# The last two of seven output groups of a graph attention layer computed on Pool instead of VectorE

## The chip, the cores and the metric

One core of a Trainium2 chip runs the whole program. The metric is the device time of one execution in microseconds. Durations inside an execution come from one profiled run, whose span goes from its first to its last instruction.

## The reference

One pre-normalised graph attention layer over 12500 nodes of 128 features and 200000 edges, with 4 heads of 32 features:

```python
h = jnp.maximum(_layernorm(x, axis=-1), 0.0)
h = (h @ W_node.T).reshape(num_nodes, H, HD)
e = (edge_features @ W_edge.T).reshape(num_edges, H, HD)
att = leaky_relu(sum(concat(h[src], h[tgt], e) * a))
m = jnp.maximum(segment_max(att, tgt), 0.0)
ex = jnp.exp(att - m[tgt])
denom = segment_sum(ex, tgt) + (num_edges - deg)[:, None] * jnp.exp(-m)
h_prime = segment_sum((ex / denom[tgt])[:, :, None] * h[src], tgt)
return x + h_prime.reshape(num_nodes, H * HD)
```

## The kernel before

The nodes are padded to 98 blocks of 128 (`N_BLOCKS`), one node per partition in each block. The program has three stages, each an `nc.Block()` in which every engine has a list of instructions written out by hand, ordered between engines by semaphores alone.

- **Stage 1** (lines 130 to 593) normalises and projects the nodes, writes a table of node rows to HBM, and lays the edges out in 1664 slots. Pool clears buffers here: some small `memset` calls and one of `vals` at the start (lines 234 to 242), one of 2375 words a partition (L248) and one of 11188 (L253). VectorE makes the statistics (`BN_STATS`, L275 and others), copies projected rows out of PSUM (L292) and computes what the slots need.
- **Stage 2** (lines 612 to 1125) goes through 52 groups of 32 slots. Pool issues an indirect DMA per slot that gathers source rows (L722), VectorE makes the scores, running maxima and weighted rows, TensorE sums them by node (L802), and VectorE adds each sum to `acc` (L1092). `acc` holds for each block a row of 137 words: per head 32 weighted sums, the sum of weights and the weight of the zero score, and after the four heads the node's degree.
- **Stage 3** (lines 1128 to 1175) is where the change lies. VectorE makes the denominators from `acc` (L1159 to L1165) and their reciprocals (L1167) in `den`, a part of `vals`. Then it goes through `N_OUT` = 7 groups of 14 blocks: it multiplies the group's sums in `acc` by the reciprocals, broadcast over the 32 features of a head, into `y`, a part of `onehot_b` (L1170), and adds `y` to that group's piece of `x`, in place (L1174). Each piece is 128 partitions by 1792 words, 896 KB.

The pieces of x lie in `x_again[g]`, buffers of stage 2 that are free by then: groups 0 and 1 in `eattr`, 2, 3, 5 and 6 in `gath`, 4 in `onehot_b`. Groups 0 to 4 are loaded from SyncE's queue (SP) before stage 2 ends, groups 5 and 6 at the start of stage 3 (L1145). ScalarE's queue (ACT) stores each group after its addition (L1151) and waits at the end for all seven stores. Pool has no instruction in stage 3. A semaphore wait stands between each two of VectorE's instructions here (`s_m`, `s_y`), since each reads what the one ahead wrote.

Of the kernel before, what the change touches and what calls it, by code (L numbers as in the profile page):

```python
# [13 lines left out]
HEADS, HD = 4, 32  # L14
P = 128
# [14 lines left out]
HC = HD + 2  # L30
# [13 lines left out]
def gat_kernel(nc, x, tiles, tile_ends, ea, w_node, w_edge, a, out):  # L44
    f32, bf16, i32 = mybir.dt.float32, mybir.dt.bfloat16, mybir.dt.int32
    ALU = mybir.AluOpType
# [10 lines left out]
    with ctx:  # L57
# [6 lines left out]
        def sem(name):  # L64
            return ctx.enter_context(nc.semaphore(name))
# [3 lines left out]
        acc_b = acc[:, :].rearrange("p (b c) -> p b c", c=ACC)  # L69
# [60 lines left out]
        with ExitStack() as stage:  # L130
            def ssem(name):
                return stage.enter_context(nc.semaphore(name))

            def ssb(name, shape, dt):
                return stage.enter_context(nc.sbuf_tensor(name, shape, dt))
# [38 lines left out]
            span, real, cnt, tot, before, end, slot_block, block, block128, same_block, unit, carry_in = (t13[:, i, :] for i in range(12))  # L174
# [19 lines left out]
            with nc.Block() as block_:  # L194
                @block_.sync
                def _(sp):
                    def load(g):
                        if g >= XBUF:
                            sp.wait_ge(n_["hn"], g - XBUF + 1)
                        sp.dma_start(xg[g % XBUF], x_g[g, :, :, :]).then_inc(s_x[g % XBUF], 16)  # L200

                    def store(g):
                        sp.wait_ge(n_["rows_act"], g + 1)
                        sp.wait_ge(n_["rows_dve"], g + 1)
                        sp.dma_start(tab_g[g, :, :, :], rows[:, g % 2, :, 0:ROW]).then_inc(s_rows[g % 2], 16)

                    sp.dma_start(ends_i[:, :, :], tile_ends).then_inc(s_ends, 16)
                    for g in range(XBUF):
                        load(g)
                    for g in range(N_NODE_GROUPS):  # L210
                        if g + XBUF < N_NODE_GROUPS:
                            load(g + XBUF)
                        if g == 2:
                            sp.wait_ge(s_block, 1)
                            sp.dma_start(slot_blocks.rearrange("(c p) -> p c", p=P), block_i[:, :], allow_slow_non_contiguous=True).then_inc(s_bstored, 16)
                        if g == 4:
                            sp.wait_ge(s_bstored, 16)
                            sp.dma_start(block_row[:, :], slot_blocks.rearrange("(o n) -> o n", o=1)).then_inc(s_brow, 16)
                        if g == FLAGS_AT:
                            sp.wait_ge(s_flags, 1)  # L220
                            sp.dma_start(flags.rearrange("e (c q) (s x) -> (q s) (e c) x", q=CG, x=4),
                                         chunk_flags[:, :, :, :].rearrange("p e c x -> p (e c) x")).then_inc(s_flags_out, 16)
                        store(g)
                    for q in range(2):
                        sp.wait_ge(s_rows[q], 16 * (N_NODE_GROUPS // 2))
                    sp.wait_ge(s_flags_out, 16)
                    sp.wait_ge(s_brow, 16)
# [270 lines left out]
                def _(pe):  # L498
# [96 lines left out]
        OW = 2 * NODE_GROUP  # L595
        N_OUT = N_BLOCKS // OW
        EARLY = 5
        FLAT = OW * NODE_DIM
        row_half = G * ROW
        x_again = [ea_flat[:, 0:FLAT], ea_flat[:, FLAT:2 * FLAT], gath_flat[:, 0:FLAT], gath_flat[:, FLAT:2 * FLAT],  # L600
                   oh_flat[:, 0:FLAT], gath_flat[:, row_half:row_half + FLAT], gath_flat[:, row_half + FLAT:row_half + 2 * FLAT]]
        x_again = [t.rearrange("p (w d) -> p w d", w=OW) for t in x_again]
        x_out = x.rearrange("(g i p) d -> g p i d", i=OW, p=P)
        s_again = [sem(f"x_again{g}") for g in range(N_OUT)]
# [9 lines left out]
        with ExitStack() as stage:  # L614
# [38 lines left out]
            with nc.Block() as block:  # L653
                @block.sync
                def _(sp):
# [35 lines left out]
                    def finish(g):  # L691
                        sp.wait_ge(s["vals"], 2 * g.n)
                        for n in range(2, EARLY - 1):
                            sp.dma_start(x_again[n], x_out[n, :, :, :]).then_inc(s_again[n], 16)
                        sp.wait_ge(s["cast"], 2 * NB * g.n)
                        sp.dma_start(x_again[EARLY - 1], x_out[EARLY - 1, :, :, :]).then_inc(s_again[EARLY - 1], 16)

# [234 lines left out]
                def _(dve):  # L932
# [128 lines left out]
                    def load_blocks(g, a):  # L1061
                        blocks = []
                        for part in range(GS // 8):
                            _, b = nc.values_load_multi_w_load_instructions(
                                block_row[:, ds(g.n * G + a * GS + 8 * part, 8)], engines=[mybir.EngineType.DVE], min_val=0,
                                max_val=N_BLOCKS, skip_runtime_bounds_check_because="clamped to N_BLOCKS in stage 1")
                            blocks += b
                        return blocks
# [59 lines left out]
        with ExitStack() as stage:  # L1128
            def ssem(name):
                return stage.enter_context(nc.semaphore(name))  # L1130

            def ssb(name, shape, dt):
                return stage.enter_context(nc.sbuf_tensor(name, shape, dt))

            y = oh_flat[:, G * P // 2:G * P // 2 + FLAT].rearrange("p (w d) -> p w d", w=OW)
            y_flat = oh_flat[:, G * P // 2:G * P // 2 + FLAT]
            den, inv = (vals_flat[:, n * 512:n * 512 + N_BLOCKS * HEADS] for n in range(2))
            den3, inv3 = (t.rearrange("p (b h) -> p b h", h=HEADS) for t in (den, inv))
            s_e, s_d, s_r, s_m, s_y, s_out = (ssem(n) for n in ("empty_nodes", "denominators", "reciprocals", "normalised", "results", "stored"))
            out_g = out.rearrange("(g i p) d -> g p i d", i=OW, p=P)  # L1140
            with nc.Block() as block:
                @block.sync
                def _(sp):
                    for g in range(EARLY, N_OUT):
                        sp.dma_start(x_again[g], x_out[g, :, :, :]).then_inc(s_again[g], 16)  # L1145

                @block.scalar
                def _(act):
                    for g in range(N_OUT):
                        act.wait_ge(s_y, g + 1)  # L1150
                        act.dma_start(out_g[g, :, :, :], x_again[g]).then_inc(s_out, 16)  # L1151
                    act.wait_ge(s_out, 16 * N_OUT)

                @block.vector
                def _(dve):
                    V = nc.vector
                    a_all = acc_b[:, 0:N_BLOCKS, 0:HEADS * HC].rearrange("p b (h c) -> p b h c", h=HEADS)
                    others = y_flat[:, 0:N_BLOCKS]
                    V.tensor_scalar(others, acc_b[:, 0:N_BLOCKS, HEADS * HC], -1.0, float(N_EDGES), ALU.mult, ALU.add).then_inc(s_e, 1)  # L1159
                    dve.wait_ge(s_e, 1)  # L1160
                    V.tensor_tensor(inv3, a_all[:, :, :, HD + 1], others.unsqueeze(2).broadcast_to((P, N_BLOCKS, HEADS)), ALU.mult).then_inc(s_e, 1)  # L1161
                    dve.wait_ge(s_e, 2)
                    V.tensor_tensor(den3, a_all[:, :, :, HD], inv3, ALU.add).then_inc(s_d, 1)  # L1163
                    dve.wait_ge(s_d, 1)
                    V.scalar_tensor_tensor(out=inv, in0=den, scalar=0.0, in1=den, op0=ALU.is_equal, op1=ALU.add).then_inc(s_d, 1)  # L1165
                    dve.wait_ge(s_d, 2)
                    V.reciprocal(den, inv).then_inc(s_r, 1)  # L1167
                    dve.wait_ge(s_r, 1)
                    for g in range(N_OUT):
                        V.tensor_tensor(y.rearrange("p b (h c) -> p b h c", h=HEADS), a_all[:, g * OW:(g + 1) * OW, :, 0:HD],  # L1170
                                        den3[:, g * OW:(g + 1) * OW, :].unsqueeze(3).broadcast_to((P, OW, HEADS, HD)), ALU.mult).then_inc(s_m, 1)
                        dve.wait_ge(s_m, g + 1)
                        dve.wait_ge(s_again[g], 16)
                        V.tensor_tensor(x_again[g], y, x_again[g], ALU.add).then_inc(s_y, 1)  # L1174
                        dve.wait_ge(s_y, g + 1)
# [34 lines left out]
```

## Time and profile before

| | us |
|---|---|
| median of 3 runs (2319.57 to 2323.26) | 2321.58 |
| the profiled execution | 2322.31 |
| its span, first to last instruction | 2320.5 |
| outside its span | 1.81 |
| stage 3 from its first instruction at 2281.4 to the span's end | 39.1 |

The engines are VectorE (DVE in the rows), ScalarE (ACT), GpSimd (POOL), SyncE (SP) and TensorE (PE, with its weight loads as PEld). A name with q behind it is an engine's queue, where DMAs are issued: the time of such a row is that of issuing, not of the transfer. A group of instructions is named by its line, its engine, its operation, what it writes and what it reads, by the program's buffer names: `onehot_b<-acc,vals` on L1170 is the product `y`, and `gath<-onehot_b,gath` on L1174 the sum with a piece of x.

### The profile page before, as it was taken

The numbers are of one execution on the slowest core, as the hardware profiler recorded it, in microseconds if no ns is written. First come the engines' busy times: TensorE is split into PE (matmuls) and PEld (weight loads), VectorE is DVE, ScalarE is ACT, GpSimd is POOL, SyncE is SP. The second block draws the span as 40 slices with busy tenths as digits, with TensorE's granted clock in tenths as the row PEclk, the third lists the DMA queues.
The fourth block names the chain that finished last, engine by engine and source line by source line (L and its number), as shares of the span: only waits on it lengthen the run. The fifth ranks groups of instructions, "written<-read, shape, count | busy, mean of one in ns | idle before, by whom it ended". The sixth has DMA issues, their size and how long they took to land. (4 is left out here: it accounts for less than half of the span.)

```text
span 2320.5 us, 28553 instructions
## 1 busy us (share of the span) xinstructions
PE 1202.7 (52%) x8210; PEld 996.3 (43%) x8210; DVE 1610.4 (69%) x4470; ACT 620.6 (27%) x1185; POOL 1623.3 (70%) x1711
## 2 busy tenths in 40 slices
PE   4465535555545546455455556555455554454441
PEld 4433434444444434444444344444344444443441
DVE  7426757767767767677677677677676776776777
ACT  5613212222222222222122222222222221222220
POOL 3077777777777777777777777777777777777730
PEclk9777677677767767767677777677677776666665
DMA  6554233233333333323233323323333222223235
GB/s 118 117 188 125 73 77 93 75 84 87 82 89 74 93 78 93 77 73 94 77 93 74 96 74 93 78 74 93 77 93 77 76 56 57 55 55 89 55 77 143
DMA packets 126702, 200.45 MB, mean 86 GB/s; under 512 B 35409, under 2 KB 92401, under 8 KB 120274
## 3 DMA queue, kind: packets, MB, share of 16 engines
q0 software_dynamic: 54912, 117.69, 22.0%
q1 hardware_dynamic: 58098, 74.36, 10.7%
q10 hardware_dynamic: 13536, 6.56, 1.0%
q8 instruction: 68, 1.11, 0.2%
q14 instruction: 88, 0.72, 0.1%
HBM read 182.18 MB, written 16.32 MB: 86 GB/s over the span
## 5 line engine op out<-in xcount | busy, mean ns | idle before, releaser
L722 POOL DMA_INDIRECT gath<-node_table,src_i x1664 | 1581.0, 950 | 512.3 <-issue 500.1
L802 PE MATMUL bank<-vals,onehot 128*128 128x137 f32 x3328 | 704.4, 390 | 537.6 <-DVE vals L1058 354.5
L802 PEld LDWEIGHTS bank<-vals,onehot 128*128 128x128 f32 x3328 | 650.6, 285 | 568.8 <-DVE vals L1058 366.4
L1092 DVE TENSOR_TENSOR acc<-acc,bank 128x137 f32 x1664 | 495.9, 298 | 506.8 <-PE bank L802 237.8
L871 ACT COPY onehot_t<-ps_oht 128x2048 bf16<-128x2048 bf16 x104 | 194.0, 1865 | 999.4 <-PE ps_oht L772 952.1
L772 PE MATMUL ps_oht<-ident_b,onehot_b 128*128 128x128 bf16 x1664 | 172.1, 286 | 328.4 <-DVE onehot_b L944 328.4
L880 ACT CAST onehot<-onehot_b 128x384 f32<-128x384 bf16 x624 | 269.2, 475 | 247.9 <-PE bank L802 242.3
L772 PEld LDWEIGHTS ps_oht<-ident_b,onehot_b 128*128 128x128 bf16 x1664 | 156.1, 135 | 337.1 <-DVE onehot_b L944 332.8
L1054 DVE TENSOR_TENSOR vals<-gath,bank 128x2048 f32<-128x2048 f32 x104 | 237.2, 2280 | 0.3 <-ACT bank L884 0.3
L944 DVE TENSOR_TENSOR onehot_b<-bank,rel_s 128x2048 bf16<-128x2048 f32 x104 | 237.2, 2282 | 0.0
L756 PE MATMUL bank<-eattr,w_eatt 128*32 128x512 f32 x392 | 184.0, 614 | 7.2 <-DMA eattr<-edge_attr_in 5.1
L756 PEld LDWEIGHTS bank<-eattr,w_eatt 128*32 128x32 f32 x392 | 40.1, 112 | 114.2 <-issue 104.7
L785 PEld LDWEIGHTS bank<-tgt_slot,onehot_t 128*128 128x128 bf16 x1664 | 55.0, 96 | 58.5 <-issue 36.1
L785 PE MATMUL bank<-tgt_slot,onehot_t 128*128 128x12 bf16 x1664 | 61.3, 183 | 19.6 <-ACT onehot_t L871 19.6
L764 PE MATMUL bank<-ident,edge_s 128*128 128x128 f32 x52 | 13.7, 416 | 104.1 <-DMA edge_s<-edge_scores,edge_idx 104.1
L992 DVE COPY chunk_max<-ends_t 4x64 f32<-4x64 f32 x208 | 54.7, 263 | 6.6
L253 POOL MEMSET acc<- 128x11188 f32 x1 | 9.4, 9422 | 70.2 <-PE bank L571 70.2
L857 ACT COPY edge_out<-bank 32x512 f32<-32x512 f32 x49 | 28.1, 574 | 112.4 <-PE bank L756 112.4
L1014 DVE COPY ends_back<-chunk_out 4x64 f32<-4x64 f32 x208 | 51.6, 248 | 4.9
L764 PEld LDWEIGHTS bank<-ident,edge_s 128*128 128x128 f32 x52 | 9.0, 211 | 105.9 <-issue 105.9
L861 ACT CAST tgt_slot<-bank 128x384 bf16<-128x384 f32 x52 | 24.9, 478 | 105.9 <-PE bank L743 103.7
L1078 DVE TENSOR_TENSOR acc<-acc,alpha 128x136 f32 x52 | 15.7, 301 | 50.1 <-issue 50.1
(170 smaller groups left out, 1005.0 us busy)
## 6 DMA issues: line engine op xcount, KB each, us to landing
eattr<-edge_attr_in SPq DMA_DIRECT2D x49, 1024.0 KB
gath<-node_table,src_i POOLq DMA_INDIRECT x1664
node_table<-onehot_b SPq DMA_DIRECT2D x14, 462.0 KB, 4.3
gath<-x_in SPq DMA_DIRECT2D x14, 448.0 KB, 5.6
gath<-x_in SPq DMA_DIRECT2D x4, 896.0 KB, 7.0
out_dram<-gath ACTq DMA_DIRECT2D x4, 896.0 KB, 4.6
edge_scores<-edge_out SPq DMA_DIRECT2D x49, 64.0 KB, 1.7
eattr<-x_in SPq DMA_DIRECT2D x2, 896.0 KB, 7.4
```

What stands on the lines that cost most here:

```text
L722: nc.gpsimd.indirect_dma_start(out=gath[:, g.r, a * GS + j, :], out_offset=None, in_=table, in_offset=bass.IndirectOffsetOnAxis(ap=src_i[: ...
L756: last = T.matmul(ps_edge, w_eatt[:, c, :], eattr[:, t % 2, c, :], start=(c == 0), stop=(c == 3))
L772: last = T.transpose(ps_oht[:, j, :], onehot_b[:, g.r, a * GS + j, :], ident_b[:, :])
L785: last = T.matmul(ps_te[:, 3 * HEADS * slot:3 * HEADS * (slot + 1)], onehot_t[:, j, :], tgt_slot[:, :, slot], start=True, stop=True)
L802: last = T.matmul(SUM_BANK[b % 3][:, (j % 3) * ACC:(j % 3 + 1) * ACC], onehot[:, b % 3, j % 3, :], vals[:, j, :], start=True, stop=True)
L871: S.copy(onehot_t[:, :, :], ps_oht[:, :, :]).then_inc(s["oht"], 1)
L880: S.copy(onehot[:, b % 3, 0:w, :], onehot_b[:, g.r, a * GS + j:a * GS + j + w, :]).then_inc(s["cast"], 1)
L944: V.tensor_tensor(onehot_b[:, g.r, a * GS:(a + 1) * GS, :], ps_iota.unsqueeze(1).broadcast_to((P, GS, P)), rel_s[:, ds(g.n * G + a * GS, G ...
L992: V.tensor_copy(chunk_max[:, :].rearrange("p (e x) -> p e x", e=2)[:, :, q:q + 4 * C - 3:4], ends_t[q * C:q * C + HEADS, :].rearrange("p ( ...
L1014: V.tensor_copy(ends_back[q * C:q * C + HEADS, :].rearrange("p (e c) -> p e c", e=2), chunk_out[:, :].rearrange("p (e x) -> p e x", e=2)[: ...
L1054: V.tensor_tensor(vh[:, :, :, 0:HD], gath[:, g.r, a * GS:(a + 1) * GS, 0:NODE_DIM].rearrange("p s (h c) -> p s h c", h=HEADS), half_of(ps_ ...
L1092: V.tensor_tensor(a_blk, a_blk, SUM_BANK[(j // 3) % 3][:, (j % 3) * ACC:(j % 3 + 1) * ACC], ALU.add).then_inc(s["added"], 1)
```

## The change

A constant `ON_VECTOR` = 5 splits the seven groups. VectorE's loop and ScalarE's stores stop after group 4. Pool gets instructions in stage 3: after the reciprocals it multiplies groups 5 and 6 in place in `acc`, then adds each product to its piece of x in `gath`. SyncE stores these two pieces and waits for both. The work on groups 0 to 4 is as before.

```diff
@@ -595,6 +595,7 @@
         EARLY = 5
+        ON_VECTOR = 5
         FLAT = OW * NODE_DIM
@@ -1137,19 +1138,38 @@
+            s_pool_m, s_pool_y, s_pool_out = (ssem(n) for n in ("pool_normalised", "pool_results", "pool_stored"))
             out_g = out.rearrange("(g i p) d -> g p i d", i=OW, p=P)
             with nc.Block() as block:
                 @block.sync
                 def _(sp):
                     for g in range(EARLY, N_OUT):
                         sp.dma_start(x_again[g], x_out[g, :, :, :]).then_inc(s_again[g], 16)
+                    for g in range(ON_VECTOR, N_OUT):
+                        sp.wait_ge(s_pool_y, g - ON_VECTOR + 1)
+                        sp.dma_start(out_g[g, :, :, :], x_again[g]).then_inc(s_pool_out, 16)
+                    sp.wait_ge(s_pool_out, 16 * (N_OUT - ON_VECTOR))
+
+                @block.gpsimd
+                def _(pool):
+                    pool.wait_ge(s_r, 1)
+                    for g in range(ON_VECTOR, N_OUT):
+                        mine = acc_b[:, g * OW:(g + 1) * OW, 0:HEADS * HC].rearrange("p b (h c) -> p b h c", h=HEADS)[:, :, :, 0:HD]
+                        pool.tensor_tensor(mine, mine, den3[:, g * OW:(g + 1) * OW, :].unsqueeze(3).broadcast_to((P, OW, HEADS, HD)), ALU.mult).then_inc(s_pool_m, 1)
+                    for g in range(ON_VECTOR, N_OUT):
+                        mine = acc_b[:, g * OW:(g + 1) * OW, 0:HEADS * HC].rearrange("p b (h c) -> p b h c", h=HEADS)[:, :, :, 0:HD]
+                        pool.wait_ge(s_pool_m, g - ON_VECTOR + 1)
+                        pool.wait_ge(s_again[g], 16)
+                        x4 = x_again[g].rearrange("p b (h c) -> p b h c", h=HEADS)
+                        pool.tensor_tensor(x4, mine, x4, ALU.add).then_inc(s_pool_y, 1)
+                    pool.wait_ge(s_pool_y, N_OUT - ON_VECTOR)
 
                 @block.scalar
                 def _(act):
-                    for g in range(N_OUT):
+                    for g in range(ON_VECTOR):
                         act.wait_ge(s_y, g + 1)
                         act.dma_start(out_g[g, :, :, :], x_again[g]).then_inc(s_out, 16)
-                    act.wait_ge(s_out, 16 * N_OUT)
+                    act.wait_ge(s_out, 16 * ON_VECTOR)
@@ -1166,7 +1186,7 @@
                     V.reciprocal(den, inv).then_inc(s_r, 1)
                     dve.wait_ge(s_r, 1)
-                    for g in range(N_OUT):
+                    for g in range(ON_VECTOR):
```

The end of VectorE's list before, from the reciprocals (`vals<-vals`) on:

```order
L1167 RECIPROCAL vals<-vals 128x392
L1170 TENSOR_TENSOR onehot_b<-acc,vals 128x1792
L1174 TENSOR_TENSOR eattr<-onehot_b,eattr 128x1792
L1170 TENSOR_TENSOR onehot_b<-acc,vals 128x1792
L1174 TENSOR_TENSOR eattr<-onehot_b,eattr 128x1792
L1170 TENSOR_TENSOR onehot_b<-acc,vals 128x1792
L1174 TENSOR_TENSOR gath<-onehot_b,gath 128x1792
L1170 TENSOR_TENSOR onehot_b<-acc,vals 128x1792
L1174 TENSOR_TENSOR gath<-onehot_b,gath 128x1792
L1170 TENSOR_TENSOR onehot_b<-acc,vals 128x1792
L1174 TENSOR_TENSOR onehot_b<-onehot_b 128x1792
L1170 TENSOR_TENSOR onehot_b<-acc,vals 128x1792
```

The list goes on with the addition of group 5 and the two instructions of group 6. Now it ends with the addition of group 4 (L1190 and L1194 are L1170 and L1174 of before):

```order
L1190 TENSOR_TENSOR onehot_b<-acc,vals 128x1792
L1194 TENSOR_TENSOR gath<-onehot_b,gath 128x1792
L1190 TENSOR_TENSOR onehot_b<-acc,vals 128x1792
L1194 TENSOR_TENSOR onehot_b<-onehot_b 128x1792
L1143 UNCONDITIONAL_BRANCH
```

Four of VectorE's fourteen large instructions are gone. The end of Pool's list now, behind the last gather of stage 2:

```order
L723 DMA gath<-node_table,src_i 128x132 x96
L654 UNCONDITIONAL_BRANCH
L1153 UNCONDITIONAL_BRANCH
L1158 TENSOR_TENSOR acc<-acc,vals 128x14x4x32 x2
L1164 TENSOR_TENSOR gath<-acc,gath 128x1792 x2
L1143 UNCONDITIONAL_BRANCH
```

Before, Pool's list ended with the gathers. The four instructions stand there as two products and two sums, and every one has two inputs in SBUF.

## Rows read from the trace of the kernel before

**Rows 1.** The page: the span, and each engine's busy time.

```profile
span 2320.5 us, 28553 instructions
PE 1202.7 (52%) x8210; PEld 996.3 (43%) x8210; DVE 1610.4 (69%) x4470; ACT 620.6 (27%) x1185; POOL 1623.3 (70%) x1711
```

**Rows 2.** The chain of waits, last pieces: start in us, us, what.

```profile
2311.42 2.04 DVE onehot_b L1170
2313.45 0.02 issue
2313.48 2.02 DVE gath L1174
```

**Rows 3.** Timeline, stage 3: start, us, engine, line, operation, tiles, count.

```profile
2284.07 2.60 DVE L1167 RECIPROCAL vals<-vals 128x392 f32<-128x392 f32 x1
2286.71 2.02 DVE L1170 TENSOR_TENSOR onehot_b<-acc,vals 128x1792 f32<-128x1792 f32 x1
2288.77 2.02 DVE L1174 TENSOR_TENSOR eattr<-onehot_b,eattr 128x1792 f32<-128x1792 f32 x1
...
2307.30 2.02 DVE L1170 TENSOR_TENSOR onehot_b<-acc,vals 128x1792 f32<-128x1792 f32 x1
```

**Rows 4.** Line L1151, the stores: durations of issuing, and time to landing.

```profile
L1151 ACTq DMA_DIRECT2D out_dram<-gath x4: 377/378/378, 2299.1 to 2315.5; - x4
DMA to landing us min/median/max: 4.6/4.6/4.6
```

**Rows 5.** DMA of stage 3, 2281.4 to 2320.5, in 40 slices.

```profile
DMA  0489999900399919991999279955997299909991
GB/s 8 119 250 348 300 290 290 259 21 0 95 291 290 264 35 291 290 291 33 276 290 289 84 213 289 291 146 150 290 290 209 91 290 290 268 27 292 292 289 39
```

**Rows 6.** Pool's groups by line and form: busy us, mean ns of one, idle.

```profile
L253 POOL MEMSET acc<- 128x11188 f32 x1 | 9.4, 9422 | 70.2 <-PE bank L571 70.2
L242 POOL MEMSET vals<- 128x2192 f32 x1 | 1.9, 1914 | 0.0
```

**Rows 7.** Timeline, 43 to 46 us: VectorE beside Pool's memset of 2375 words.

```profile
43.45 2.09 POOL L248 MEMSET acc<- 128x2375 f32 x1
...
43.48 2.09 DVE L275 TENSOR_SCALAR st<-mv 128x7 f32<-128x7 f32 x1
43.56 2.01 DVE L292 COPY onehot_b<-bank 128x408 f32<-128x408 f32 x1
```

**Rows 8.** Line L275: min/median/max duration in ns of its 14 instructions.

```profile
L275 DVE TENSOR_SCALAR st<-mv x14: 170/171/2093, 9.0 to 103.5; 128x7 f32<-128x7 f32 x14
```

**Rows 9.** Timeline, 2.7 to 5.9 us: Pool's last memsets, and VectorE.

```profile
2.54 0.52 POOL L241 MEMSET flag_row<- 4x516 f32 x1
...
3.84 1.91 POOL L242 MEMSET vals<- 128x2192 f32 x1
...
2.74 3.05 DVE L312 TENSOR_SCALAR ends_i<-ends_i 128x26 int32<-128x26 int32 x1 [0.44 <-DMA ends_i<-tile_ends_in]
5.83 0.18 DVE L313 CAST ends_f<-ends_i 128x26 f32<-128x26 int32 x1
```

**Rows 10.** Timeline, 112 to 132 us: VectorE's copies from PSUM during L253's memset.

```profile
118.87 0.58 DVE L292 COPY onehot_b<-bank 128x408 f32<-128x408 f32 x1 [7.04 <-PE bank L517]
122.26 0.58 DVE L292 COPY onehot_b<-bank 128x408 f32<-128x408 f32 x1 [2.51 <-PE bank L517]
```

**Rows 11.** Line L253: when its one memset of 9422 ns began.

```profile
L253 POOL MEMSET acc<- x1: 9422/9422/9422, 115.8 to 115.8; 128x11188 f32 x1
```

## The prediction

> **What bounds the kernel now.** I read four views. The page's first lines [rows 1] show that no engine is busy throughout, so a stage has to be read by itself, and only stage 3 is touched. The chain of waits [rows 2] shows stage 3's end: VectorE's instructions follow one another with 0.02 us between them, and the last ends at 2315.50 us. The timeline of the stage [rows 3] gives the pace: the first product starts at 2286.71 us, right behind the reciprocals, and a large instruction takes 2.02 us and starts 2.059 us after the last; 14 of them fill 2286.71 to 2315.50 us. The stores [rows 4] hide under this work except the last: it is issued at 2315.5 us, lands 4.6 us later, and 0.4 us more ends the span at 2320.5 us. So stage 3 is a chain on VectorE plus one exposed store of 5.0 us. The DMA view [rows 5] shows what the stores leave: while one moves, the core gets about 290 GB/s and the engines stand at nine tenths or more, and between two of them they fall idle. One piece is 128 x 1792 x 4 bytes = 0.9175 MB, so it needs 3.16 us of the 4.11 us that VectorE takes per group.
>
> **What the change removes.** Four of VectorE's 14 instructions, 4 x 2.059 = 8.24 us. VectorE alone would end at 2286.71 + 10 x 2.059 - 0.03 = 2307.27 us. ScalarE issues two stores fewer; each took 0.38 us of issue beside other work, so nothing is gained from that.
>
> **What it adds on Pool.** Four instructions of 1792 words a partition. No row has a two-input operation of Pool. Its memsets [rows 6] cost 9422 ns / 11188 = 0.84 ns a word for one access to SBUF (the smaller one, 1914 / 2192, gives 0.87). A product or sum needs two reads and a write. If the write hides behind the reads it is two accesses, 2 x 0.84 x 1792 = 3.0 us, with 0.1 us to start 3.1; if nothing hides it is three, 4.5 + 0.1 = 4.6 us. No row is nearer to one end than to the other, so I take the middle, 3.85 us, and 15.4 us for four. The Trainium skill, GPSIMD Engine Reference, Performance versus the Vector engine, gives 4497 ns for such an addition of 2048 words; scaled to 1792 words that is an estimate of 3.93 us, and by it the sum below would be 0.3 us longer.
>
> The product is now made in place in `acc`, in runs of 32 words, as VectorE reads it at the same 2.02 us as the dense addition [rows 3]; I cost the shape at nothing. Pool's queue is empty in this stage, and its last gather was issued long before, so nothing waits behind Pool's wait for the reciprocals. On SyncE the two loads of x stand ahead of the new stores and have no wait; the stores queue behind them, and nothing behind the stores.
>
> **Whether the two engines run side by side.** This decides the sign. Rows of before show one engine held by the other for whole instructions. At 43.48 us VectorE's L275, on 7 words, took 2.09 us and ended at 45.57, 0.03 us after Pool's memset of 43.45 to 45.54 [rows 7]; the other instructions of that line take 0.171 us at the median [rows 8]. At 2.74 us L312, on 26 words, took 3.05 us and ended at 5.79, 0.04 us after the last of a run of memsets that Pool issued without a wait between them [rows 9]: VectorE got no turn between Pool's instructions. Against that, VectorE's copies out of PSUM took 0.58 us each [rows 10] inside the memset of 115.8 to 125.2 us [rows 11], unhindered. So what is held is access to SBUF by some forms of instruction, and not all. After the change, from 2286.7 us on, both engines have only instructions with two SBUF inputs, and all of Pool's also write SBUF. No row has VectorE's two-input form beside a busy Pool. The bounds are: nothing is held, or each instruction excludes the other engine's.
>
> I take exclusion, since held rows are those with operands in SBUF and the free rows the ones from PSUM. The Trainium skill, SBUF — State Buffer, SBUF: two separate sides, says that a VectorE instruction with two SBUF inputs and a Pool instruction that reads SBUF want the same read interface, and that the one that starts first keeps it to its end. That is the case of this change and speaks against it; the held rows agree with a lock for whole instructions, but only for one-input forms, and no run here yet shows the two-input form.
>
> **The sum.** Under exclusion the order of turns doesn't matter, since one engine works at a time: 10 x 2.059 + 15.4 = 36.0 us where before there were 14 x 2.059 = 28.8. That is +7.2 us. An instruction that was held has done its start already (L275 ended 0.03 us after release and not 0.171, so 0.14 us is hidden [rows 7, 8]); with some three changes of turn that is -0.4 us. The last store's 5.0 us remains, from whichever engine is last: stores come at least 3.85 us apart and each needs 3.16. Result +6.8 us: VectorE or Pool ends at 2322.3 us, the span at 2327.3, the profiled execution would take 2329.1 us. The median of the runs shown lies 0.7 us under the profiled one; against it the forecast is 2321.6 + 6.8 = **2328.4 us**.
>
> **The rivals.**
> - **Side by side, and faster.** If neither engine is held, Pool ends its sums at 2286.7 + 3 x 3.85 = 2298.3 and 2302.1 us, and VectorE at 2307.27. For it: the free rows [rows 10]. Against: the held rows. The gain isn't 8.2 us, since the stores then become the bound. Each needs 1.4 us ahead of its data (4.6 - 3.16). Data of the second store ends at about 2299.5 us; then five follow without a pause, 5 x 3.16 = 15.8, and the last lands at 2315.3, or 2315.7 with small gaps. Before, it landed at 2320.1. So -4.4 us, 2317.2. It decides for faster only if Pool is not held at all and a store keeps to 3.16 us or less (the best slice has 348 GB/s [rows 5]).
> - **Sharing word by word.** If the engines take turns within an instruction, the shared way carries VectorE's second input, 10 x 1.9 us, and Pool's two, 4 x 3.0 us: 31 us at the least against 28.8, +2 us, 2323.6. Nothing in the rows shows a VectorE instruction merely stretched by a part; the two held ones were held to the end. But they are of another form.
> - **Pool far dearer than its bound.** If runs of 32 words or a first use of the instruction cost Pool more, at 6 us each the sum under exclusion is 10 x 2.059 + 24 - 28.8 = +15.8 us, 2337. The same price alone, side by side, would end Pool at 2310.7, and the change would be about the same as before.
> - That the change doesn't do what it says is excluded by the engines' lists: the four instructions stand on Pool.
>
> **How the numbers follow.** A measurement of this kernel can tell about 0.2%, 4.6 us, from no change. Exclusion gets 0.60, side by side 0.20, sharing 0.15, a far dearer Pool 0.05. Exclusion with Pool at 3.1 us gives 4 x 3.1 - 8.2 - 0.4 = +3.8 us, 2325.4, and at 4.6 us +9.8, 2331.4; only its lowest part lies within 0.2%, so 0.55 slower and 0.05 same. A dearer Pool adds 0.05 to slower. Sharing is same. Side by side lies on the bound: 0.11 faster and 0.09 same. Together: slower 0.60, same 0.29, faster 0.11. The likeliest case's own range is 2325.4 to 2331.4. To hold 8 in 10 the range must reach down to side by side, so it goes from 2317.0 to 2332.0 and leaves out a dearer Pool and the best of the gains.
>
> **What the changed profile would show.** Under exclusion: instructions of L1190 and L1194 that take 2.02 us or, where held, 2.02 us and what is left of Pool's instruction, up to 5.9 us, and one of up to 17 us if Pool issues its four without giving a turn; busy time of VectorE from 2286.7 us on near 36 us for ten instructions; the last store issued at about 2322.3 us. Side by side: all ten at 2.02 us and the last of VectorE at 2307.27, stores that take more than 4.6 us to land, and no idle slice in the DMA view. Sharing: instructions of 3 us or so with no jump. The forecast is wrong if VectorE's instructions beside Pool's keep to 2.02 us, and its size is wrong if Pool's, undisturbed, start less than 3.1 or more than 4.6 us apart.

## The result, and the profile after

The change makes the kernel slower by a little: 2326.52 us at the median of 22 runs against 2321.86 us for the kernel before (22 runs). The ratio on record is 1.0016 with a 95% interval of 1.0010 to 1.0023, or about 3.7 us (2.3 to 5.3); the two medians by themselves lie 4.66 us apart. The time lies inside the range given, 1.9 us under the 2328.4 us that were forecast. The likeliest case, exclusion, is the one that came, but its price was set too high: 6.8 us were forecast. The loss is clear of the noise. At 0.16% it stays under the 0.2% that bounded "slower"; by the medians alone, 0.20%, it lies on that bound.

The profiled execution took 2326.59 us, with a span of 2324.7 us. Stage 3 is best compared by itself, from SyncE's first load to the span's end: 2320.5 - 2281.41 = 39.09 us before, 2324.7 - 2281.31 = 43.39 us after, 4.30 us more.

The page of the kernel after, which answers to [rows 1]:

```profile
span 2324.7 us, 28554 instructions
PE 1205.2 (52%) x8209; PEld 999.2 (43%) x8210; DVE 1616.0 (70%) x4466; ACT 620.6 (27%) x1185; POOL 1644.0 (71%) x1715
```

VectorE has four instructions fewer and is busy 5.6 us longer. Of this 4.4 us fall in stage 3, where it is held inside its instructions. The timeline of stage 3 after shows where (start, us, engine, line, operation, tiles, count; the neighbours of a kind are merged, as Pool's two products at 2286.66). It answers to [rows 3]:

```profile
2286.61 2.02 DVE L1190 TENSOR_TENSOR onehot_b<-acc,vals 128x1792 f32<-128x1792 f32 x1
2286.66 9.98 POOL L1158 TENSOR_TENSOR acc<-acc,vals 128x1792 f32<-128x1792 f32 x2 [51.95 <-DVE vals L1187]
2288.67 4.91 DVE L1194 TENSOR_TENSOR eattr<-onehot_b,eattr 128x1792 f32<-128x1792 f32 x1
...
2293.61 4.92 DVE L1190 TENSOR_TENSOR onehot_b<-acc,vals 128x1792 f32<-128x1792 f32 x1
2296.61 10.87 POOL L1164 TENSOR_TENSOR gath<-acc,gath 128x1792 f32<-128x1792 f32 x2
2298.56 5.39 DVE L1194 TENSOR_TENSOR eattr<-onehot_b,eattr 128x1792 f32<-128x1792 f32 x1
...
2303.98 5.39 DVE L1190 TENSOR_TENSOR onehot_b<-acc,vals 128x1792 f32<-128x1792 f32 x1
2309.40 2.02 DVE L1194 TENSOR_TENSOR gath<-onehot_b,gath 128x1792 f32<-128x1792 f32 x1
```

The two engines take strict turns. VectorE's first product runs at once; Pool's first, which starts at 2286.66 in the profile, shows 5.04 us because it waits for that. Then each of VectorE's next four takes 4.91, 4.92, 5.39 and 5.39 us: 2.02 of its own and the rest of one Pool instruction. From 2309.40 us on Pool is done and the other five take 2.02 us again. The delays add to 2.89 + 2.90 + 3.37 + 3.37 = 12.5 us; less the 8.24 us of the four instructions taken away that is +4.3 us, the whole difference of the stage.

The chain of waits ends as in [rows 2], on VectorE, now with group 4 at 2317.64:

```profile
2317.62 0.02 issue
2317.64 2.02 DVE onehot_b L1194
```

The last store follows it, with the same 5.0 us to the span's end. The stores of Pool's groups lay long before that, so SyncE's queue costs nothing here.

### The profile page after: what moved, and what is told of

Read it like the earlier page. It is cut to its first block and busy times, and to the rows that moved or that the text cites. A ratio compares the mean times of both kernels' runs of the same rounds, so it can differ in the third digit from the quotient of the medians.

```text
span 2324.7 us, 28554 instructions
## 1 busy us (share of the span) xinstructions
PE 1205.2 (52%) x8209; PEld 999.2 (43%) x8210; DVE 1616.0 (70%) x4466; ACT 620.6 (27%) x1185; POOL 1644.0 (71%) x1715
## 5 line engine op out<-in xcount | busy, mean ns | idle before, releaser
L253 POOL MEMSET acc<- 128x11188 f32 x1 | 9.4, 9427 | 70.0 <-PE bank L571 70.0
```

## The experiments

**Nothing overlapped (e1).** VectorE waits for Pool's last sum before its first product.

```diff
+                    dve.wait_ge(s_pool_y, N_OUT - ON_VECTOR)
                     for g in range(ON_VECTOR):
```

> VectorE waits for Pool's two sums before its first product, so nothing of the two engines can overlap. Exclusion (my theory): in the changed kernel nothing overlapped either, so only the four hidden starts of 0.14 us are lost and Pool's start is added: Pool's four instructions alone take 3.06 + 3.06 + 3.53 + 3.53 = 13.2 us plus starts, VectorE's ten 20.6 us, the last of VectorE ends near 2321 us instead of 2319.7, the span is 0.5 to 2 us longer than the changed kernel's. Sharing word by word: Pool's instructions alone would be clearly shorter than the stretches I read from the changed kernel (under 2.5 us for a product) and the whole shorter than or equal to the changed kernel's.

Measured: stage 3 takes 3379.6 - 3334.84 = 44.76 us, 1.4 us more than in the changed kernel, and VectorE ends 39.7 us after the stage's start, not 38.35. Making the two engines fully serial costs only 1.4 us, so nearly nothing ran side by side in the changed kernel, and exclusion stands. The price of Pool's instructions with nothing beside them can be read here too:

```profile
3340.20 6.38 POOL L1158 TENSOR_TENSOR acc<-acc,vals 128x1792 f32<-128x1792 f32 x2 [72.05 <-DVE vals L1187]
3346.53 7.32 POOL L1164 TENSOR_TENSOR gath<-acc,gath 128x1792 f32<-128x1792 f32 x2
3353.95 2.03 DVE L1191 TENSOR_TENSOR onehot_b<-acc,vals 128x1792 f32<-128x1792 f32 x1 [13.84 <-POOL gath L1164]
```

Products take 3.2 us and sums 3.7 us, 13.75 us for the four. The ratio to the kernel before was 1.0033 (1.0014 to 1.0053). On the chip of e1 to e4 every kernel, that of before too, took about 1.45 times as long (before: 3365 us); stage 2 was slower there, for a reason not looked into, and stage 3 kept its pace (VectorE's large instructions 2.02 us, one store 290 GB/s), so these four are compared by their stage 3. The kernel before was profiled only on the first chip; the stage 3 that each later run is compared with is the one of that trace, 39.09 us.

**Only the products with one input in PSUM (e2).** The reciprocals are copied to PSUM, and VectorE's products read them there; its sums still read two inputs in SBUF.

```diff
-        bank = [pb(f"bank{i}", [P, 512]) for i in range(6)]
+        banks = pb("banks", [P, 6 * 512])
+        bank = [banks[:, i * 512:(i + 1) * 512] for i in range(6)]
...
+            den_p = banks[:, 4 * 512:4 * 512 + N_BLOCKS * HEADS]
...
-                    V.reciprocal(den, inv).then_inc(s_r, 1)
+                    V.reciprocal(den, inv).then_inc(s_d, 1)
+                    dve.wait_ge(s_d, 3)
+                    V.tensor_copy(den_p, den).then_inc(s_r, 1)
...
-                                        den3[:, g * OW:(g + 1) * OW, :]
+                                        den_p3[:, g * OW:(g + 1) * OW, :]
```

> The reciprocals are copied to PSUM (0.5 us) and VectorE's products read them there, so a product has one SBUF input and a sum still has two. If the second SBUF input is what collides: the products beside Pool take 2.02 us, the sums stay held, VectorE ends near 2312 us and the span ends near 2318 us, 2 us less than before. If any SBUF access of VectorE collides with Pool: products and sums are both held as in the changed kernel, the span is that of the changed kernel plus 0.5 us.

Measured: the two lines of VectorE in this kernel, products and sums, with min/median/max duration in ns:

```profile
L1195 DVE TENSOR_TENSOR onehot_b<-acc,banks x5: 2020/2021/2021, 3342.3 to 3363.3; 128x1792 f32<-128x1792 f32 x5
L1199 DVE TENSOR_TENSOR eattr<-onehot_b,eattr x2: 2877/2986/3094, 3344.4 to 3349.6; 128x1792 f32<-128x1792 f32 x2
L1199 DVE TENSOR_TENSOR gath<-onehot_b,gath x2: 3340/3347/3354, 3354.5 to 3360.0; 128x1792 f32<-128x1792 f32 x2
```

No product is held; each sum beside Pool is held by 0.9 to 1.3 us, what is left of Pool's instruction when the product has passed beside it. VectorE ends 31.0 us after the stage's start (34.1 before), and the stage takes 37.7 us, 1.4 us less than before. It doesn't gain the whole 3.1 us, since the last store, issued at 3367.45 us, takes 6.65 us to the span's end and not 5.0: others are still moving ahead of it. What collides in these forms is VectorE's second input in SBUF, not its access to SBUF as such. The ratio, 0.9995 (0.9971 to 1.0019), can't tell 1.4 us.

**Products and sums with one input in PSUM (e3).** As e2, and `y` lies in PSUM too.

```diff
+            y_p = banks[:, 0:FLAT].rearrange("p (w d) -> p w d", w=OW)
...
-                        V.tensor_tensor(x_again[g], y, x_again[g], ALU.add).then_inc(s_y, 1)
+                        V.tensor_tensor(x_again[g], y_p, x_again[g], ALU.add).then_inc(s_y, 1)
```

> The reciprocals and the product y lie in PSUM, so no large instruction of VectorE has two SBUF inputs. If the second SBUF input is what collides: all ten take 2.02 to 2.1 us, VectorE ends near 2307.8 us, Pool's products take about 3.1 and its sums 3.5 us undisturbed, and the stores become the bound: the DMA view has no idle slice, the last store lands near 2316 us, the span is 4 us shorter than before (ratio 0.9983). If the writes or any SBUF access collide too: VectorE's instructions beside Pool's take about 5 us again and the span is that of the changed kernel.

Measured: the groups of its stage 3 by line and form (busy us, mean ns, idle):

```profile
L1196 DVE TENSOR_TENSOR banks<-acc,banks 128x1792 f32<-128x1792 f32 x5 | 10.1, 2029 | 0.2
L1168 POOL TENSOR_TENSOR gath<-acc,gath 128x1792 f32<-128x1792 f32 x2 | 7.3, 3694 | 0.0
L1162 POOL TENSOR_TENSOR acc<-acc,vals 128x1792 f32<-128x1792 f32 x2 | 6.4, 3218 | 72.6 <-DMA gath<-x_in 72.6
L1200 DVE TENSOR_TENSOR gath<-banks,gath 128x1792 f32<-128x1792 f32 x2 | 4.0, 2024 | 0.1
```

Both engines now run at their own pace, side by side. VectorE ends 26.5 us after the stage's start, 7.6 us earlier than before, but the stage takes 3352.2 - 3316.71 = 35.5 us, only 3.6 us less. The DMA view of this stage in 40 slices, to be held against [rows 5], says why:

```profile
DMA  0389999970005999099999999999999999999990
GB/s 9 94 234 334 333 288 292 288 192 13 0 0 163 288 291 282 10 267 290 261 281 290 254 279 268 291 282 274 289 287 291 288 262 299 289 286 291 291 282 10
```

From the second store on no slice is idle (the last digit is the span's end). The stores are the bound, as the rival "side by side" had it. The ratio was 0.9985 (0.9962 to 1.0007), not told from 1 on this chip.

**Pool's prices alone (e4, e10).** Sixteen and fourteen Pool instructions behind VectorE's last sum, one at a time, on buffers that are free; they add their own time to these two kernels (one run each, 3425.44 and 2374.51 us) and don't touch the output. The core of e4:

```diff
+                    pool.wait_ge(s_y, N_OUT)
+                    for _ in range(2):
+                        step(pool.tensor_tensor(sums(0), sums(0), spread(0), ALU.mult))
+                        step(pool.tensor_tensor(sums(1), sums(1), spread(1), ALU.add))
+                        step(pool.tensor_tensor(sums(2), sums(2), x4, ALU.mult))
+                        step(pool.tensor_tensor(sums(3), sums(3), x4, ALU.add))
+                        step(pool.tensor_tensor(y, y, x_again[6], ALU.mult))
+                        step(pool.tensor_tensor(y, y, x_again[6], ALU.add))
+                        step(pool.tensor_tensor(y2, y2, x2, ALU.add))
+                        step(pool.tensor_copy(y, x_again[6]))
```

`sums(g)` is a group's part of `acc`, in runs of 32 words; `spread(g)` the broadcast reciprocals; `y` and x are dense.

> The kernel before, and behind VectorE's last sum sixteen Pool instructions on the same shapes, one after the other with waits, with no VectorE work beside them (the output is already being stored; they only write buffers that are free). Two reads through one port: a product or sum of 1792 words with both inputs full size costs about 3.5 us, one with the broadcast reciprocals about 3.1 us (its second input is 56 words a partition, held over 32 words), whatever the operation. If the operation decides instead: the products cost 3.1 us and the sums 3.5 us whatever the operands. A copy of 1792 words costs about half of a sum.

Pool's groups in e4 (busy us, mean ns of one; lines 1167 to 1174 are the eight steps in order):

```profile
L1173 POOL TENSOR_TENSOR onehot_b<-onehot_b,gath 128x2048 f32<-128x2048 f32 x2 | 9.0, 4494 | 0.2
L1171 POOL TENSOR_TENSOR onehot_b<-onehot_b,gath 128x1792 f32<-128x1792 f32 x2 | 7.9, 3955 | 0.2
L1172 POOL TENSOR_TENSOR onehot_b<-onehot_b,gath 128x1792 f32<-128x1792 f32 x2 | 7.9, 3954 | 0.2
L1169 POOL TENSOR_TENSOR acc<-acc,gath 128x1792 f32<-128x1792 f32 x2 | 7.4, 3684 | 0.2
L1170 POOL TENSOR_TENSOR acc<-acc,gath 128x1792 f32<-128x1792 f32 x2 | 7.4, 3680 | 0.2
L1168 POOL TENSOR_TENSOR acc<-acc,vals 128x1792 f32<-128x1792 f32 x2 | 6.4, 3211 | 0.2
L1174 POOL COPY onehot_b<-gath 128x1792 f32<-128x1792 f32 x2 | 3.4, 1676 | 0.1
```

Product or sum makes no difference (L1171 and L1172, L1169 and L1170); the inputs do: 3.96 us dense, 3.68 with one input in runs, 3.21 with the broadcast one. The last two were expected 0.1 to 0.2 us cheaper, from the held instructions of the changed kernel, whose start is hidden; dense inputs, expected at the same 3.5 us as the changed kernel's sums, cost 0.45 us more than that. The copy at 1.68 us is half of a sum or less, as expected. The addition of 2048 words at 4.49 us, whose inputs are dense, agrees with the figure of the Trainium skill (GPSIMD Engine Reference, Performance versus the Vector engine, 4497 ns).

e10 asked which operand does it; its steps write dense to dense in place (L1168) and elsewhere (L1169), runs plus dense to runs (L1170) and to a dense buffer (L1171), dense plus dense to runs (L1172), runs plus runs (L1173), and a dense input times the broadcast one (L1174).

> The kernel before, and behind VectorE's last sum fourteen Pool instructions of 1792 words alone, to see what sets Pool's price (the output is already being stored). In e4 both inputs dense took 3.96 us, one in runs of 32 words in rows of 137 took 3.68, one broadcast 3.21. If two dense reads get in each other's way, two inputs in runs (acc and acc) cost 3.7 us or less, and a dense output into another buffer changes nothing. If the output's shape decides, runs to dense costs 3.96 us and dense to runs 3.68. If working in place decides, dense to another buffer is cheaper than in place.

```profile
L1172 POOL TENSOR_TENSOR acc<-onehot_b,gath 128x1792 f32<-128x1792 f32 x2 | 7.9, 3956 | 0.2
L1169 POOL TENSOR_TENSOR onehot_b<-gath 128x1792 f32<-128x1792 f32 x2 | 7.9, 3954 | 0.2
L1171 POOL TENSOR_TENSOR onehot_b<-acc,gath 128x1792 f32<-128x1792 f32 x2 | 7.3, 3667 | 0.2
L1173 POOL TENSOR_TENSOR acc<-acc 128x1792 f32<-128x1792 f32 x2 | 6.8, 3386 | 0.2
L1174 POOL TENSOR_TENSOR onehot_b<-gath,vals 128x1792 f32<-128x1792 f32 x2 | 6.4, 3206 | 0.2
```

The output's place and shape do nothing. With two inputs of full size, each one in runs of 32 words, instead of dense, takes 0.28 us off: 3.95, 3.67, 3.39. Beside the broadcast input the runs take nothing off: 3.21 us (e4, L1168) and, with the other input dense, 3.21 us too (L1174). Why reading with gaps is cheaper was not settled; the data says only that the inputs set the price.

**PSUM without Pool (e5).** As e3, with `ON_VECTOR` = 7 and Pool's and SyncE's new parts taken out again.

> VectorE makes all seven groups as before, with the reciprocals and y in PSUM; Pool has nothing in the stage. If PSUM only takes the collision away and gives no speed of its own: fourteen instructions of 2.02 us, the copy of the reciprocals adds 0.6 us, stage 3 takes 39.7 us where before it takes 39.1. If PSUM operands make VectorE itself faster: its instructions fall below 2.0 us and the gain of e3 has come from there and not from Pool.

Measured: stage 3 takes 2319.4 - 2279.66 = 39.74 us, 0.65 more than before; products take 2.03 and sums 2.02 us; ratio 0.9996 (0.9987 to 1.0005). The added copy of the reciprocals is 0.60 us of that. PSUM gives VectorE nothing by itself, so e3's gain comes from Pool running beside it.

**One group on Pool (e6).**

```diff
-        ON_VECTOR = 5
+        ON_VECTOR = 6
```

> The change with one group on Pool instead of two. Exclusion: each moved group takes 4.12 us from VectorE and gives 3.06 + 3.53 us of Pool's time to the same chain, less two hidden starts, so half of the change's loss: stage 3 about 2.1 us longer than before (41.2 us), VectorE's last instruction ends 36.2 us after the stage's start. If the loss came from both queues' stores or from Pool's start instead, it would not halve: near 0 or near 4 us.

Measured: stage 3 takes 2320.2 - 2278.92 = 41.28 us, +2.2 us, VectorE ends 36.2 us after its start, ratio 1.0007 (0.9998 to 1.0016). The timeline shows one held instruction of VectorE for each of Pool's:

```profile
2286.27 4.92 DVE L1194 TENSOR_TENSOR eattr<-onehot_b,eattr 128x1792 f32<-128x1792 f32 x1
...
2291.22 5.39 DVE L1190 TENSOR_TENSOR onehot_b<-acc,vals 128x1792 f32<-128x1792 f32 x1
...
2296.65 2.03 DVE L1194 TENSOR_TENSOR eattr<-onehot_b,eattr 128x1792 f32<-128x1792 f32 x1
```

A moved group costs 2.90 + 3.37 = 6.27 us of delay and gives back 4.12, so the loss is 2.15 us a group. It is a price per group, and no fixed cost of starting Pool or of a second store queue.

**Which forms collide (e8).** Behind VectorE's last sum, ten pairs one at a time: Pool starts, and VectorE follows 0.14 to 0.20 us later with 1792 words on other data. They too add only their own time (one run, 2365.88 us).

```diff
+                    for n, op in enumerate((both, both, both, both, both, clear, clear, clear, copy, copy)):
+                        pool.wait_ge(s_go, n + 1)
+                        op().then_inc(s_pool, 1)
...
+                    for n, op in enumerate((tt2, tt1, cps, cpp, red, tt2, tt1, cps, tt2, cps)):
```

> The kernel before, and behind its last sum ten pairs, one at a time: Pool starts an instruction, VectorE 0.3 us later starts one of 1792 words on other data (the output is already being stored). Pool's sum with two SBUF inputs (3.7 us), against VectorE's sum with two SBUF inputs: held, up to 5 us; sum with one input in PSUM: 2.0 us; copy SBUF to SBUF: held, about 4 to 5 us, since one-input forms in SBUF were held by memsets before; copy out of PSUM and reduction: not held. Pool's memset of 5376 words (4.5 us), against the sum with two SBUF inputs: not held if only Pool's reading collides with the second input, held if any Pool access does; the sum with one PSUM input: not held; the copy SBUF to SBUF: held. Pool's copy (1.7 us) against the sum: held for the rest of it.

The timeline of six of the pairs (Pool's instruction, then VectorE's):

```profile
2317.57 3.68 POOL L1157 TENSOR_TENSOR acc<-acc,gath 128x1792 f32<-128x1792 f32 x1 [83.16 <-DVE vals L1206]
...
2317.77 5.36 DVE L1198 TENSOR_TENSOR onehot_b<-onehot_b,gath 128x1792 f32<-128x1792 f32 x1
...
2323.54 3.70 POOL L1157 TENSOR_TENSOR acc<-acc,gath 128x1792 f32<-128x1792 f32 x1 [2.29 <-DVE vals L1206]
2323.68 2.02 DVE L1199 TENSOR_TENSOR onehot_b<-banks,gath 128x1792 f32<-128x1792 f32 x1
...
2327.85 4.49 DVE L1200 COPY onehot_b<-gath 128x1792 f32<-128x1792 f32 x1
...
2341.04 4.58 POOL L1158 MEMSET acc<- 128x5376 f32 x1 [0.45 <-DVE vals L1206]
...
2341.21 2.03 DVE L1198 TENSOR_TENSOR onehot_b<-onehot_b,gath 128x1792 f32<-128x1792 f32 x1
...
2351.26 5.35 DVE L1200 COPY onehot_b<-gath 128x1792 f32<-128x1792 f32 x1
...
2357.16 3.42 DVE L1198 TENSOR_TENSOR onehot_b<-onehot_b,gath 128x1792 f32<-128x1792 f32 x1
```

VectorE's durations in us, by its form and what Pool does:

| VectorE | Pool sum, 3.7 | Pool memset, 4.6 | Pool copy, 1.7 |
|---|---|---|---|
| sum, both inputs in SBUF | 5.36 held | 2.03 | 3.42 held |
| sum, one input in PSUM | 2.02 | 2.02 | |
| copy SBUF to SBUF | 4.49 held | 5.35 held | 2.47 held |
| copy PSUM to SBUF | 2.02 | | |
| reduction over SBUF | 2.02 | | |

The copies within SBUF were not timed alone, but in all three pairs they end 0.94 to 0.95 us after Pool's instruction, however long that is, so they waited for its end. So there are two kinds of collision. A sum with two SBUF inputs is held by a Pool instruction that reads SBUF and not by a memset; a copy within SBUF is held by either. The Trainium skill, SBUF — State Buffer, Who interferes with whom, says that the second SBUF input comes through the read interface shared with Pool, and that copies, among other one-input forms, can take the shared pair. The trace agrees with it in all ten pairs. Pool, which started first, kept to its own time in each pair: the second comer pays.

**A version that uses it (e7, e9).** e7 is as e3, but ScalarE copies the reciprocals to PSUM beside VectorE's first product, which reads them in SBUF.

```diff
-                    pool.wait_ge(s_r, 1)
+                    pool.wait_ge(s_rp, 1)
...
+                    act.wait_ge(s_r, 1)
+                    nc.scalar.copy(den_p, den).then_inc(s_rp, 1)
...
+                        if g == 1:
+                            dve.wait_ge(s_rp, 1)
```

> As e3, but ScalarE copies the reciprocals to PSUM beside VectorE's first product, which reads them in SBUF; Pool starts behind that copy. If the second SBUF input is what collides, Pool's first product is held by VectorE's first for about 1.5 us and nothing else is, VectorE's ten take 2.02 us, and stage 3 ends with the stores: 34.9 us, 4.2 us less than before (ratio about 0.998). If the stores are not the bound in e3, the stage would follow VectorE's last instruction, 26 us after the stage's start, plus 5 us: 31 us.

Measured: 2318.86 us at the median, ratio to before 0.9981 (0.9972 to 0.9990). Stage 3 takes 2320.1 - 2284.84 = 35.26 us, not 34.9. Pool's first product is held by VectorE's first, which started before it, by 1.3 us (the two products take 7.70 us and not 6.4), and none of VectorE's is held: here too the second comer pays. VectorE ends 25.9 us after the stage's start; the stores are the bound again. The DMA view (40 slices of the stage) shows the 0.4 us that are missing as a dent behind the second store, since Pool's first store comes only 17.25 us after the stage's start:

```profile
GB/s 9 73 254 346 323 290 291 290 204 9 0 40 293 289 291 127 142 290 290 289 113 269 289 290 293 241 281 290 287 290 291 285 280 288 288 287 289 290 276 10
```

So e9 lets Pool finish group 5 before it multiplies group 6: the second loop's header is taken out, and product and sum of a group stand together.

```diff
-                    for g in range(ON_VECTOR, N_OUT):
-                        mine = acc_b[:, g * OW:(g + 1) * OW, 0:HEADS * HC].rearrange("p b (h c) -> p b h c", h=HEADS)[:, :, :, 0:HD]
                         pool.wait_ge(s_pool_m, g - ON_VECTOR + 1)
```

> As e7, but Pool finishes group 5 before it starts on group 6, so its first store is issued about 14.0 us after the stage's start and not 17.3, and the DMA engines have no gap behind the second store. If the stores are the bound: the last six follow from 14.9 us on, 6 x 3.16 us, and stage 3 takes 34.8 us where e7 takes 35.3. If they are not the bound: the stage stays at 35.3 us, since VectorE's and Pool's work is the same. Either way the kernel is faster than before by 4 us or more (ratio near 0.998).

Measured: 2318.08 us at the median of 11 runs, ratio 0.9978 (0.9969 to 0.9987), the lowest ratio of all. Its stage 3 takes 2316.0 - 2281.11 = 34.89 us, 4.2 us less than before and 8.5 less than the changed kernel. The times of e7 and e9 aren't told apart by the runs. In the one trace of each, e9's stage is 0.37 us shorter, with Pool's first store at 14.2 us:

```profile
2291.59 3.68 POOL L1167 TENSOR_TENSOR gath<-acc,gath 128x1792 f32<-128x1792 f32 x1
...
2295.30 7.32 SPq L1155 DMA_DIRECT2D out_dram<-gath  x2
```

## Why the prediction was right, and where its size was off

- **What bounds stage 3.** Right: VectorE's chain and one store. VectorE's five instructions ahead of the products, its last five behind Pool's, and the 5.0 us at the end kept the durations read from [rows 3, 4].
- **Exclusion.** Right, and shown three ways: the strict turns in the changed kernel, e1's mere 1.4 us for forbidding overlap, and e2, e3 and e8, where the collision of these forms goes away when VectorE's second input leaves SBUF (2.02 us beside Pool's sum) or when Pool's instruction reads nothing from SBUF (2.03 us beside its memset). The sharing within an instruction that the second rival supposed is ruled out: VectorE's instruction waits whole and then runs at its own pace.
- **The forecast's reason for exclusion** was weaker than its result. It took from [rows 7, 9, 10, 11] that operands in SBUF are held and operands in PSUM are not. e8 shows that the held rows are of the other kind: memsets hold one-input forms in SBUF, and would not have held a two-input sum (2.03 us). What tied the change's own forms together was the rule of the Trainium skill, SBUF — State Buffer, SBUF: two separate sides, not those rows. [rows 7] also has a copy out of PSUM (L292) at 2.01 us, which the forecast passed over. It ended with L275, at 45.57 us, and stands behind it in VectorE's order, so most likely it waited for L275 and not for Pool; alone it takes 0.58 us even during a memset [rows 10].
- **Pool's price.** The larger of two mis-sized terms of the sum. I took the middle of two and three accesses, 3.85 us each, 15.4 us; measured alone they are 3.21 and 3.68 us, 13.8 us for the four. The estimate of 3.93 us by the figure of the Trainium skill (GPSIMD Engine Reference, Performance versus the Vector engine) would have been further off; e4 and e10 found such a price, 3.95 us, only with dense inputs. I cost the shape at nothing because VectorE doesn't feel it; Pool does, downward, through the broadcast reciprocals and the runs in `acc`. That is 1.6 us of the miss.
- **Hidden starts.** The second mis-sized term. I allowed 0.4 us for three changes of turn. There were four held instructions of VectorE, and each was delayed by 0.32 us less than Pool's instruction takes alone (3.21 - 2.89, 3.68 - 3.37), 1.3 us together. The trace shows the parts: in each turn VectorE's instruction ends 1.88 to 1.89 us after Pool's end, where it takes 2.02 alone; Pool's ends 3.06 or 3.54 us after VectorE's end, where it takes 3.21 or 3.68 alone; and the 0.04 us between two instructions of VectorE, in which Pool runs already, are no part of the delay. So about 0.14 us of both engines is hidden in every turn, where I had counted one engine's for three turns. That is 0.9 us of the miss. With both put right the sum is 13.8 - 1.3 - 8.24 = +4.3 us, which is stage 3's difference.
- **The profile of the change.** I had allowed for one held instruction of up to 17 us, since Pool gave no turn between its memsets in [rows 9]. It gave one after each instruction here, and none of VectorE's took more than 5.39 us.
- **Side by side.** It didn't come, but its arithmetic was tested by e3, e7 and e9: with the collision gone the gain was 3.6, 3.8 and 4.2 us of the 8.2 taken from VectorE, against 4.4 worked out. The stores take the rest.
- **The chances.** 0.60 stood on slower by over 0.2%, 0.29 on within 0.2%. At +0.16% by the ratio the latter came, narrowly, and through the price, not through another mechanism; most of the 0.29 stood on sharing and side by side, which didn't come. The case's own lower end had Pool at 3.1 us, and the truth, 3.45 at the mean, was much nearer to it than to the upper one.

## What to carry to other kernels

Moving elementwise work from VectorE to Pool gained nothing here while both read two inputs from SBUF: the two take turns, and Pool's instruction is 1.6 to 1.8 times as long as the one that it replaces. Put one of VectorE's inputs in PSUM first (here the product and the reciprocals, at no cost in its pace), and then share the work. Before that, work out what becomes the bound: at 290 GB/s the seven stores allowed half of the 8.2 us taken from VectorE, and from then on what counts is how early each store can start.

## What the runs showed of the hardware that was not expected

- Pool's two-input instruction of 1792 words costs 3.95 us with dense inputs, 3.67 with one input in runs of 32 words, 3.39 with both, and 3.21 with a broadcast input, whether the other is dense or in runs; output and operation don't matter. The cause is open.
- Two engines that collide take strict turns here, one instruction each, though VectorE starts the next within 0.04 us of the last. In [rows 9], with memsets on Pool, VectorE waited through a whole run of them: seven in the trace, from the one at 2.54 us to the one at 3.84 us. What decides between turns and no turns was not tried.
- The duration that the profile shows for a held instruction includes its wait, for Pool as for VectorE: Pool's products show 5.0 us in the changed kernel and 3.2 alone. Busy time under a collision is no measure of work.
